# Own slot tables for the last ticks of a fused attention and FFN kernel, other queues for the first loads

## The reference, cut to what matters

```python
k = (x @ Wk.T).reshape(B, S, H, Dh).transpose(0, 2, 1, 3)   # B=2, S=4096, H=16, Dh=32
v = (x @ Wv.T) ...
k = k * cos + _rotate_half(k) * sin
def step(W, kv):                       # 256 steps of 16 tokens, W0 = identity
    kc, vc = kv
    z = einsum('bhsd,bhde->bhse', kc, W)
    grad = einsum('bhsd,bhse->bhde', kc, (z - vc) * inv_n)
    return (W - LR * grad, z)
_, zs = lax.scan(step, W0, (k_c, v_c))
attn = layernorm(out, gamma, beta) @ Wo.T
x = layernorm(x + attn)
g = (x @ gate_w.T) * gate_s            # gate_w, up_w: (1408, 512), ternary
u = (x @ up_w.T) * up_s
x = layernorm(x + ((silu(g) * u) @ down_w.T) * down_s)
```

## Time and profile before

| what | value |
|---|---|
| median of 3 runs | 1948.31 us (1947.62 to 1955.94) |
| profiled execution | 1948.8 us, its span 1946.7 us |
| TensorE busy | 1856.2 us, 95% of the span |
| VectorE, ScalarE, GpSimd busy | 1185.3, 550.7, 652.1 us |
| mean granted TensorE clock | 0.982 of full speed |

### The profile page before, as it was taken

How to read it: one execution, slowest core, us unless ns; L and a number is a source line. 1 busy time by engine, 2 the same in 40 slices (tenths; PEclk the granted TensorE clock), 3 DMA queues, 4 the chain that set the end, 5 groups by cost and what they waited for, 6 DMA issues and landing times.

```text
span 1946.7 us, 60662 instructions
## 1 busy us (share of the span) xinstructions
PE 1856.2 (95%) x25784; PEld 1482.0 (76%) x25784; DVE 1185.3 (61%) x2602; ACT 550.7 (28%) x1238; POOL 652.1 (33%) x783
## 2 busy tenths in 40 slices
PE   7868999999999999999999999999999999888897
PEld 5647787787778778877877777777777777767776
DVE  3655666666666566666666666666666665555543
ACT  3212323232222223222232223233322322222222
POOL 2222333333333333333333333333333333323333
PEclk9978999999999999999999999999999999999999
DMA  8974444554544554554455454445545544443310
GB/s 282 289 225 136 149 138 144 168 155 142 157 147 135 148 163 143 159 149 132 143 161 165 134 155 148 137 145 166 159 141 154 151 126 135 124 123 110 101 61 23
DMA packets 310783, 288.29 MB, mean 148 GB/s; under 512 B 43376, under 2 KB 261616, under 8 KB 310512
## 3 DMA queue, kind: packets, MB, share of 16 engines
q1 hardware_dynamic: 297840, 266.57, 45.9%
q10 hardware_dynamic: 12672, 17.83, 2.8%
HBM read 153.17 MB, written 139.72 MB: 150 GB/s over the span
## 4 chain that ended last, share of the span: by engine, by line
PE 80%; DVE 10%; DMA 4%; SPq 2%; ACT 2%; issue 1%; ACTq 0%; POOL 0%; POOLq 0%; DVEq 0%
PE gu_acc L973 32%; PE work L954 25%; PE down_acc L987 13%; PE scan_acc L926 4%; PE scan_acc L943 4%; DVE x_tok L1153 2%; DMA landed<-x1T_scr 2%; DVE state L1233 2%; DVE hid L1238 2%; DVE turned L1158 2%; SPq L327 1%; ACT hid L689 1%; PE scan_acc L973 1%; SPq L372 1%; PE down_acc L954 1%
## 5 line engine op out<-in xcount | busy, mean ns | idle before, releaser
L579 POOL TENSOR_TENSOR hid_lo<-hid,hid_hi 128x256 fp32r<-128x256 f32 x352 | 262.6, 746 | 644.3 <-ACT hid_hi L699 644.2
L973 PE MATMUL gu_acc<-x_hi,gw 128*128 128x256 f32 x1372 | 379.5, 309 | 11.4 <-DVE hid L1238 5.8
L689 ACT ACTIVATE hid<-gu_acc,gate_scale 128x256 f32<-128x256 f32 x343 | 162.7, 474 | 780.8 <-PE gu_acc L973 780.5
L1238 DVE SCALAR_TENSOR_TENSOR hid<-gu_acc,up_scale,hid 128x256 f32<-128x256 f32 x343 | 165.6, 483 | 317.6 <-ACT hid L689 317.4
L973 PE MATMUL gu_acc<-x_lo,gw 128*128 128x256 f32 x1372 | 343.5, 283 | 0.0
L973 PE MATMUL gu_acc<-x_hi,uw 128*128 128x256 f32 x1372 | 341.4, 281 | 0.0
L973 PE MATMUL gu_acc<-x_lo,uw 128*128 128x256 f32 x1372 | 340.4, 281 | 0.0
L1233 DVE SCALAR_TENSOR_TENSOR state<-scan_acc,half_step,state 128x256 f32<-128x256 f32 x512 | 223.3, 477 | 165.9 <-PE scan_acc L943 161.2
L973 PEld LDWEIGHTS gu_acc<-x_hi,gw 128*128 128x128 f32 x1372 | 261.1, 190 | 48.2 <-DVE hid L1238 21.8
L987 PE MATMUL down_acc<-dw,hid_hi 128*128 128x512 f32 x704 | 282.3, 401 | 2.3 <-POOL hid_lo L579 2.2
L987 PE MATMUL down_acc<-dw,hid_lo 128*128 128x512 f32 x704 | 279.1, 396 | 0.0
(11 more groups left out here) (129 smaller groups left out, 2251.6 us busy)
## 6 DMA issues: line engine op xcount, KB each, us to landing
x_fm<-xT SPq DMA_DIRECT2D x64, 256.0 KB, 3.5
k_rows<-k_scr SPq DMA_DIRECT2D x512, 32.0 KB, 2.0
z_scr<-v_rows SPq DMA_DIRECT2D x32, 512.0 KB, 3.2
z_tok<-z_scr SPq DMA_DIRECT2D x512, 32.0 KB, 1.8
x_tok<-x SPq DMA_DIRECT2D x32, 512.0 KB, 5.7
v_rows<-v_scr SPq DMA_DIRECT2D x496, 32.0 KB, 2.0
out<-x_tok SPq DMA_DIRECT2D x31, 512.0 KB, 2.8
kT_scr<-turned SPq DMA_DIRECT2D x120, 128.0 KB, 2.9
```

What stands on the lines that cost most here:

```text
L579: pool.tensor_tensor(hid_lo[m % RING][:], hid[m % 2], hid_hi[m % RING][:].bitcast(F32), ALU.subtract).then_inc(hid_lo_ready, 1)
L689: act.activation(hid[m % 2], gu_bank(n, m)[:, 0:TOK], ACT.Silu, scale=gate_scale[:, m:m + 1]).then_inc(silu_done, 1)
L973: mm = pe.matmul(gu_bank(n, m)[:, k * TOK:(k + 1) * TOK], lhsT=w[:, c, m * P:(m + 1) * P].bitcast(dt), rhs=part[:, c].bitcast(dt), start=( ...
L1238: dve.scalar_tensor_tensor(hid[m % 2], gu_bank(n, m)[:, TOK:2 * TOK], up_scale[:, m:m + 1], hid[m % 2], ALU.mult, ALU.mult).then_inc(hid_r ...
```

## The change

- New tables `TURNING` (tick 29) and `LATE` (ticks 30 to 32); `WITHOUT_SCAN` changes with them. In ticks 30 to 32 all 11 pieces of tile t-3 run in the tick, pieces 0 to 7 in slots 0 to 7 and the others in slots 10 to 12; tick 29 runs pieces 2 to 10 of tile 26 and none of tile 27. Tick 33 has all 11 pieces of tile 30.
- In ticks 29 to 32 (`late(t)`) the steps of tile t-2 stand later: statistics of z slot 1, `normalize` 2, `turn_zn` 3, `high_zn`, `low_zn` and `add_bias` 7, `project_o` 8 and 9, `add_o` 9 and 10, `normalize` and `turn_x1` 11, `high_x1` and `low_x1` 15.
- x of tiles 3 to 6 is loaded by ScalarE: tile 3 in slot 7 of tick 1, tiles 4 and 5 in slot 15, tile 6 in slot 4 of tick 2.
- z of tile 0 is read in tick 2 by one call, behind the second half of tile 1's rows and `store_v(3, 0)`.
- Some stores, weight copies and loads, `weigh` pieces, `turn_k(5)` and steps of x of tile 3 change their places in ticks 1 and 2.

```diff
+USUAL, TURNING, LATE, WITHOUT_SCAN, END = None, NT - LEAD, NT - LEAD + 1, NT + 1, NT + 2
 GATE_UP = {USUAL: {14: (2, 0), 15: (2, 1), 0: (3, 2), 2: (3, 3), 3: (3, 4), 5: (3, 5), 7: (3, 6), 8: (3, 7), 9: (3, 8),
                    10: (3, 9), 11: (3, 10)},
-           WITHOUT_SCAN: {0: (3, 2), 1: (3, 3), 2: (3, 4), 3: (3, 5), 4: (3, 6), 5: (3, 7), 6: (3, 8), 8: (3, 9),
-                          9: (3, 10), 11: (2, 0), 12: (2, 1), 13: (2, 2), 14: (2, 3), 15: (2, 4)},
+           TURNING: {0: (3, 2), 1: (3, 3), 2: (3, 4), 3: (3, 5), 4: (3, 6), 5: (3, 7), 6: (3, 8), 7: (3, 9), 10: (3, 10)},
+           LATE: {0: (3, 0), 1: (3, 1), 2: (3, 2), 3: (3, 3), 4: (3, 4), 5: (3, 5), 6: (3, 6), 7: (3, 7), 10: (3, 8),
+                  11: (3, 9), 12: (3, 10)},
+           WITHOUT_SCAN: {0: (3, 0), 1: (3, 1), 2: (3, 2), 3: (3, 3), 4: (3, 4), 5: (3, 5), 6: (3, 6), 7: (3, 7), 8: (3, 8),
+                          9: (3, 9), 10: (3, 10), 11: (2, 0), 12: (2, 1), 13: (2, 2), 14: (2, 3), 15: (2, 4)},
...
-        WITHOUT_SCAN: {0: (3, 1), 1: (3, 2), 2: (3, 3), 3: (3, 4), 4: (3, 5), 5: (3, 6), 7: (3, 7), 8: (3, 8), 9: (3, 9),
-                       10: (3, 10), 12: (2, 0), 13: (2, 1), 14: (2, 2), 15: (2, 3)},
+        TURNING: {0: (3, 1), 1: (3, 2), 2: (3, 3), 3: (3, 4), 4: (3, 5), 5: (3, 6), 6: (3, 7), 7: (3, 8), 8: (3, 9),
+                  11: (3, 10)},
+        LATE: {1: (3, 0), 2: (3, 1), 3: (3, 2), 4: (3, 3), 5: (3, 4), 6: (3, 5), 7: (3, 6), 8: (3, 7), 11: (3, 8),
+               12: (3, 9), 13: (3, 10)},
+        WITHOUT_SCAN: {1: (3, 0), 2: (3, 1), 3: (3, 2), 4: (3, 3), 5: (3, 4), 6: (3, 5), 7: (3, 6), 8: (3, 7), 9: (3, 8),
+                       10: (3, 9), 11: (3, 10), 12: (2, 0), 13: (2, 1), 14: (2, 2), 15: (2, 3)},
...
-WEIGHED = {(1, 5): (0,), (1, 8): (1,), (1, 11): (2,), (1, 13): (3,), (2, 0): (4,), (2, 2): (5,), (2, 4): (6,), (2, 6): (7,),
-           (2, 9): (8,), (2, 10): (9,), (2, 11): (10,), (2, 13): (11,)}
...
+       TURNING: DOWN[TURNING], LATE: DOWN[LATE], WITHOUT_SCAN: DOWN[WITHOUT_SCAN], END: DOWN[END]}
+WEIGHED = {(1, 6): (0,), (1, 10): (1,), (1, 13): (2,), (2, 0): (3,), (2, 2): (4,), (2, 4): (5,), (2, 6): (6,), (2, 9): (7,),
+           (2, 10): (8,), (2, 11): (9,), (2, 12): (10,), (2, 13): (11,)}
...
+def late(t):
+    return NT - LEAD <= t <= NT
...
-    age, m = table.get(t, table[USUAL]).get(s, (0, -1))
+    age, m = table.get(LATE if late(t) and t != TURNING else t, table[USUAL]).get(s, (0, -1))
...
-                    load_x_fm(3)
+                    load_k_half0(1)
                     store_z(0, 0, NS // 2)
-                    load_k_half0(1)
-                    load_z(0, 0, NS // 2, 16)
                     store_v(2, 0)
+                    store_k(2)
+                    store_v(2, 1)
                     load_v_half0(1, 0)
                     load_v_half0(1, 1)
-                    store_k(2)
                     store_z(0, NS // 2, NS - 1)
-                    store_v(2, 1)
-                    load_x_fm(4)
-                    load_z(0, NS // 2, NS - 1, 32)
...
-                    load_z(0, NS - 1, NS, 48)
...
                     store_v(3, 0)
+                    load_z(0, 0, NS, 48)
                     store_k(3)
                     store_v(3, 1)
-                    load_x_fm(5)
...
-                    load_x_fm(6)
...
-                    store_z(1, 0, NS // 2)
                     store_v(5, 1)
                     load_k_half0(2)
+                    store_z(1, 0, NS // 2)
                     load_z(1, 0, NS // 2, 16)
-                    store_kT(5)
                     load_v_half0(2, 0)
                     load_v_half0(2, 1)
+                    store_kT(5)
...
+            def load_x_fm(n):
+                act.wait_ge(x_low, 2 * n)
+                for b in range(BATCH):
+                    act.dma_start(x_fm[:, :, b, :],
+                                  xT[:, b, rows(n)].rearrange("(c p) t -> p c t", p=P)).then_inc(x_fm_in, 16)
+                act.wait_ge(k_mul, 6 * (n - 1))
+                act.dma_start(rot[n % 2][:], rope[rows(n), :].rearrange("t (a d) -> t a d", a=2)
+                              ).then_inc(rot_in[n % 2], 16)
...
-                    if t == 1 and s == 9:
+                    if t == 1 and s == 7:
+                        load_x_fm(3)
+                    if t == 1 and s == 11:
                         high_x(3, 0)
                     if t == 1 and s == 13:
                         high_x(3, 1)
                     if t == 1 and s == 15:
+                        load_x_fm(4)
                         copy_v(3, 0)
                         high_x(4, 0)
                         copy_v(3, 1)
                         high_x(4, 1)
+                        load_x_fm(5)
                     if t == 2 and s == 1:
                         high_x(5, 0)
+                    if t == 2 and s == 4:
+                        load_x_fm(6)
...
-                    if within(o) and s == (12 if o != LAST else 10):
+                    if within(o) and s == (10 if o == LAST else 15 if late(t) else 12):
...
-                    if t == 1 and s == 0:
-                        load_ffn(0, 0)
-                        copy_ffn(1, 0)
-                    if t == 1 and s == 2:
...
+                    if t == 1 and s in (0, 4, 8, 12):
+                        load_ffn(0, s // 4)
+                    if t == 1 and s in (2, 6, 10, 14):
+                        copy_ffn(1, s // 4)
+                    if t == 1 and s == 15:
                         load_ffn(1, 0)
-                        copy_ffn(1, 3)
-                    if t == 1 and s == 12:
+                        copy_ffn(2, 0)
+                    if t == 2 and s == 0:
...
-                        load_ffn(2, 3)
+                    if t == 2 and s in (5, 6, 7, 8):
+                        load_ffn(2, s - 5)
...
-                    if within(o) and s in (6, 7):
-                        project_o(o, s - 6)
+                    if within(o) and s in ((8, 9) if late(t) else (6, 7)):
+                        project_o(o, s % 2)
...
-                    if within(o) and s in (7, 8):
-                        add_o(o, s - 7)
+                    if within(o) and s in ((9, 10) if late(t) else (7, 8)):
+                        add_o(o, (s + 1) % 2)
...
-                    if within(o) and z_by_dma(o) and s == 2:
+                    if within(o) and s in ((9, 10) if late(t) else (7, 8)):
+                        dve.wait_ge(o_added, 2 * o + (s + 1) % 2 + 1)
+                        stats_of(1, (s + 1) % 2, x_tok)
+                    if within(o) and z_by_dma(o) and s == (3 if late(t) else 2):
                         turn_zn(o, 0)
                         turn_zn(o, 1)
-                    if within(o) and s == (6 if o == LAST else 5):
...
+                    if t == 2 and s == 10:
                         turn_k(5, 0)
                         turn_k(5, 1)
...
-                    if within(o) and s == 9:
+                    if within(o) and s == (11 if late(t) else 9):
...
-                    if within(o) and s == (12 if o != LAST else 10):
+                    if within(o) and s == (10 if o == LAST else 15 if late(t) else 12):
                         low_x1(o, 0)
-                    if within(o) and s == (13 if o != LAST else 10):
+                    if within(o) and s == (10 if o == LAST else 15 if late(t) else 13):
                         low_x1(o, 1)
...
-                    if within(o) and s == (2 if o == 0 else 3 if o == LAST else 0):
+                    if within(o) and s == (2 if o == 0 else 3 if o == LAST else 1 if late(t) else 0):
...
-                    if within(o) and s == (3 if o == 0 else 4 if o == LAST else 1):
+                    if within(o) and s == (3 if o == 0 else 4 if o == LAST else 2 if late(t) else 1):
```

More of the change, by code:

```diff
@@ L637, in tick @@
                         add_rotated(n, 1)
-                    if within(o) and s == 4:
+                    if within(o) and s == (7 if late(t) else 4):
                         add_bias(o, 0)
@@ L802, in tick @@
                         high_hid(*unit_at(LOW, t, s))
-                    if within(o) and s == (6 if o == LAST else 5):
+                    if within(o) and s == (6 if o == LAST else 7 if late(t) else 5):
                         high_zn(o, 0)
@@ L812, in tick @@
                         save_z(sc, s // 2)
-                    if within(o) and s == (6 if o in (0, LAST) else 5):
+                    if within(o) and s == (6 if o in (0, LAST) else 7 if late(t) else 5):
                         high_zn(o, 1)
@@ L1352, in tick @@
                         normalize(1, o, 0, x1_tok[o % 2], x_tok, x1_ready)
-                    if within(o) and z_by_dma(o) and s == 9:
+                    if within(o) and z_by_dma(o) and s == (11 if late(t) else 9):
                         turn_x1(o, 0)
-                    if within(o) and s == 9:
+                    if within(o) and s == (11 if late(t) else 9):
                         normalize(1, o, 1, x1_tok[o % 2], x_tok, x1_ready)
```

(4 more changed lines are left out.)

43 lines of the change are left out of this document (9 added, 34 removed).

## The result

The changed kernel takes 1959.08 us, the median of nine runs (1957.34 to 1964.22); the kernel before took 1951.49 in nine runs beside it (1947.59 to 1955.94). The ratio is 1.0044, with the interval 1.0031 to 1.0057: 0.4% slower. The forecast was 1948, and the range ended at 1959.

What follows compares the result with a forecast made beforehand. TensorE, busy 95% of the span, was taken as the bound, with idle time at both ends. 1948.8 less 14 at the front plus 13.3 in the late ticks gave 1948.1, said as 1948; 8-in-10 range 1937 to 1959.

Steps and rivals of the forecast that it cites:

- Front, tile 5: First ticks: x of tile 5 lands before TensorE wants it; the 10.3 us wait and 2.5 us slowness go, 12.8 saved.
- Front, tile 4: First ticks: x of tile 4 lands at 76, not 79.5, and its unit takes 2.96 us, not 4.61; 5.1 saved.
- Front, what is given back: First ticks: z(0)'s read, a moved `weigh` and ScalarE's in-order waits take back 3.9 us of the 17.9 saved.
- z(0)'s read: Tick 2: the one read of z of tile 0 lands late and delays VectorE's later steps, 2.4 us, bounds 0 and 5.
- Late ticks, the loop: Ticks 29 to 32: serial latencies plus TensorE's work between them set a period of 55.3 us against 54.8.
- G of tile 27: First `gate_up` of tile 27's piece 0, claimed 55.4 us after the start of tick 29, waiting for `x_lo`.
- P to G: From the second output projection's end to the next tile's first `gate_up` of piece 0: a latency chain of 18.5 us.
- G to P: From the first `gate_up` of a tile's piece 0 to the end of the second output projection: 36.8 us.
- Late ticks, the clock: Late ticks: steps behind gaps of 2 to 5 us at four boundaries run partly at 1.2 GHz, 2.5 us added.
- Late ticks, where tick 33 begins: Tile 30's first `gate_up` comes at 1869.2, 7.1 us behind 1862.15, taken as the start of tick 33's FFN.
- That the loads on ScalarE come no earlier: Rival, first ticks: x lands behind weight copies, the front saves only 3 us, time 1959; slower case, chance 0.14.
- That the late tables cost nothing: Rival, late ticks: periods fall to 52.5 us, only the heavier tick 33 costs 3; time 1938, chance 0.18.

Runs made afterwards that it cites:

- front_only: The changed kernel with the old tables and slots of the last ticks, so only the first ticks differ from the kernel before: 1943.43 us, ratio 0.9957.
- warm: The changed kernel plus matmuls on idle operands where TensorE would stand in the late ticks: 1961.43 us, ratio 1.0039 to the kernel before.
- late_only: The kernel before with only the tables and slots of the last ticks changed: 1972.52 us, ratio 1.0098.
- warm_z_addo: `warm_z` with `add_o` ahead of `step_state` on VectorE in slot 9 of the late ticks: 1946.34 us, ratio 0.9967 to the kernel before.
- addo_first: The changed kernel with `add_o` ahead of `step_state` on VectorE in slot 9 of the late ticks: 1952.26 us, ratio 0.9997 to the kernel before.
- warm_z: `warm` with statistics, normalising and turning of z one slot later in the late ticks: 1956.67 us, ratio 1.0019 to the kernel before.
- sp_early: The kernel before with the load of x of tile 5 moved ahead on SyncE's queue, before a k store: 1950.20 us, ratio 0.9984.

## Why the prediction was wrong

The forecast was no change, and the kernel became 0.44% slower. Of the 11.0 us between 1948.1 and the median of 1959.08, 2.7 are the base (the sum was made against an execution of 1948.8, the later median of the kernel before is 1951.49), 7.6 are the loss between the two medians and 0.7 the gain that the sum had.

- *Front, tile 5: right.* 12.8 us were expected; the unit starts with no wait and takes 3.06, and its wait of 10.31 and slow unit of 5.49 are gone.
- *Front, tile 4: wrong, 3 us.* I expected 5.1. The unit ends 1.9 us earlier (84.31 for 86.23): the wait is nearly as long (4.38 for 4.68), and the unit behind it slower (5.24 for 4.61). The load went out at 67.32, 4.4 us earlier than in the earlier trace rows, but it was seen at 77.04, only 2.6 earlier than in the earlier trace rows: it took 9.7 us from issue to ScalarE instead of 7.8, with the DMA engines full (share 0.99 from 68 to 72, 1.01 from 72 to 76). Whether the weight copy issued just before it on the same queue has a part in this was not tried. TensorE, too, asked 2.2 us sooner (71.73 for 73.98), which kept the wait. The gap was not short enough for the unit behind it to keep the high clock.
- *Front, what is given back: near in size, wrong in place.* It is 2.7 us (14.7 ahead behind the unit of tile 5, 12.1 at tick 3) for 3.9. Where I had put 2.4 for z(0)'s read, the trace has three short waits, 0.38 and 0.21 for the rotation and 0.28 for `err`, 0.9 together. The wait for `x_tok`, which I let stay at 2.00, grew by 3.1, because its load waits for v stores of tiles 3 and 4. Tick 3 came 12.1 us early in the profile, for 14 predicted; over all kernels with this front it is nearer 10, and the timed gain of `front_only` is 8.4.
- *Late ticks, the loop: right as a chain, its sum partly by luck.* G of tile 27 came 54.8 us after tick 29's start (predicted 55.4), with a wait for `x_lo`; `x_tok` was waited for four times, 1.89 us at most (1.75 predicted); P to G took 17.8 to 18.1 (18.5). G to P took 39.5, 41.3 and 39.5 for 36.8. The idle time rose by 11.7 us, for the 10.8 of my sum without the clock, but the 10.8 holds a misread row (see below), and `warm`, which has the clock, still loses 23.6. The sum left out waits that the low clock covered, such as z, at 1.0 us a tick (up to 2.1 in `warm`), as far as the added matmuls are not themselves the cause.
- *Late ticks, the clock: this is the failed step.* "I add 2.5, since part of it is hidden behind the wait for z." The busy time of the same 3,469 entries rose by 11.8 us. I had priced the low clock as a tail behind gaps of 2 to 5 us at four boundaries. The new tables take the FFN pieces out of slots 14 and 15, in tick 29 out of 12 to 15, so in front of each G only short scan steps are left, and the granted clock is 0.50 for 10 us at three of the boundaries and 20 at the first. The kernel before has low stretches here as well, but shorter (mean 0.97). The term measured 11.8 for 2.5, 9.3 of the 10.1 us by which the late part was missed. As a whole it cost 23.4 us in the profile, beyond its bounds of 6 to 20, and 19 in the timed `late_only`, for 13.3.
- *Late ticks, where tick 33 begins: a misread row, and a wait that stayed.* The sum counts "7.1 behind 1862.15" as if the FFN of tick 33 began there. It is piece 1 of tile 30, in slot 15 of tick 32; piece 0 is at 1858.91 and piece 2, the first of tick 33, at 1865.38:

```profile
1858.91 0.39 PE L973 MATMUL gu_acc<-x_hi,gw 128*128 128x256 f32 x1
...
1865.38 0.39 PE L973 MATMUL gu_acc<-x_hi,gw 128*128 128x256 f32 x1
```

  Those two rows are of the kernel before. The term should have been 3.8 for 7.1, the sum without the clock 7.5 for 10.8, and the forecast 1944.8, farther from 1959. Of the idle time of 11.7 us, 4.2 were then not foreseen. 2.1 of them are the wait for z of tile 31, which the sum let go and which is there as in the earlier trace rows:

```profile
PE scan_acc L1035 <- DVE z_tok L1156: 2.1, 2, 1.4
```

- *But it is not the clock alone:* `warm` brought the clock back to 0.97 and won nothing. Its busy time, less the 20.0 us of the added matmuls, is 259.6, for 257.5 in the kernel before. What was given back went into waiting, for z in part. With the clock held, z late and the order on VectorE turned, a gain did show (`warm_z_addo`, 0.30% under `addo_first`). The traces fit a cost hidden by another: VectorE never waits for z in ticks 29 to 32 of the kernel after, 5.5 us in `warm`. The timed runs do not settle it, since `warm_z` against `warm` is not clear of noise, and neither remedy was tried alone on `addo_first`.
- *By the timed halves the front missed as much as the late ticks:* 8.4 us for 14, and 19 for 13.3. Of the front's 5.6, tile 4 is 3.2 in the profile; what the rest is was not found.
- *The rivals.* That the loads on ScalarE come no earlier: false, tile 5's load went out 18.2 us earlier. Its time, 1959, came out, but by another way. That the late tables cost nothing: false, by `late_only`.

The Trainium skill, "DMA: Bandwidth & Descriptors", section "Issuing engines are not separate DMA queues", says that a second issuing engine saves only issue time. The traces of `sp_early` and of the kernel after show what it leaves out: a load on an in-order queue waits for all that stands ahead of it, and holds up what stands behind. Moved forward on the one queue, the load took away the wait of 10.31 and brought one of 3.80. By the medians it gave 0.16%, and the front with its second queue 0.43%, but the intervals touch, and how much of the difference is the front's other edits was not tried. For tile 4 the sentence fits the trace: 4.4 us earlier out, 2.6 earlier in.

## What to carry to other kernels

When work is moved away from a place where TensorE is thinly used, price the place that is left: the engine pauses more there, and the clock of what stands there and just behind may fall, as it did here to 0.50. Compare the busy time of an unchanged set of instructions before and after, since this separates the clock from the waits in one row; but what the clock costs is only known once it has been held up in a run. Where two latencies end near each other, removing one may show nothing; remove both before judging either. Another queue helps a load only where its place on the in-order queue makes it late, and not where its transfer does.

## What the runs showed that was not expected

- Matmuls on idle operands held the granted clock at 0.97 in the late ticks for 0.91 without them, at 63 entries more; the stretch came out as long (312.1 for 311.9 us).
- The same front starts tick 3 anywhere from 151.8 to 157.4 us, in kernels that do not differ ahead of it. This spread of 5.6 us is more than most terms of the front's sum, so one profile is too few to settle them.
- The stretch from tick 29 on spreads as well: with the same tables and slots it takes 288.5 us in the kernel before, 289.4 in `front_only` and 293.7 in `sp_early`, at clocks of 0.97, 0.97 and 0.95. The 23.4 us of the case are well above this spread of 5.2, but differences of a few us between two profiles are not.
